# 36 products of a tile of ones on TensorE at the start of a two-layer gated attention kernel on one core

## Chip, core and metric

The kernel runs on one core of one Trainium2 chip. The metric is the device time in microseconds (us), median of three runs.

## The reference, cut to what matters

Eight sequences of 112 tokens (256 wide) go through two blocks; each block adds gated cross attention on a context of 375 rows and then a gated feed-forward part. All data are float32.

```python
x = x + tanh(g_xattn[0]) * L0_xattn(ctx, layernorm(x), ...)   # 8 heads of 64, rotary keys
x = x + tanh(g_ffn[0])   * L0_ffn(layernorm(x), ...)          # 8 experts, top 2, plus a shared one
x = x + tanh(g_xattn[1]) * L1_xattn(layernorm(x), ctx, ctx)   # 16 heads of 16
x = x + tanh(g_ffn[1])   * L1_ffn(layernorm(x), ...)          # gated q, k, v mix, causal attention
return x
# inside L0_xattn, for each sequence (xn: normed context, ln: normed latents)
q = (ln @ Wq) * scale
k, v = split(concat([xn, ln]) @ Wkv)
out = softmax(q @ rope(k).T) @ v @ Wo
```

The change touches only what runs before the first product of the first block. Nothing that it computes is part of the result.

## The kernel before

The program is written out by hand, one instruction stream for each engine, with counted semaphores between them. The first block's attention runs sequence by sequence (`n`, 0 to 7) and, within one, in four steps of two heads.

What happens before TensorE (PE) first works, for sequence 0:

- SyncE (SP) issues the loads: x of sequence 0, its context (`cx`, 375 KB), `ident`, `affine`, then `wkv`, `wq`, `cos_t`, `sin_t` and x of sequence 1.
- GpSimd (POOL) fills constants; `ones` (128x128) is the first (line 393), each with an increment of `s_fill`.
- VectorE (DVE) takes the statistics of the context (line 881), POOL turns them into scales (lines 416 to 419), ScalarE (ACT) normalises the context into `hat` (line 576, a tile of the `arena` buffer).
- PE waits for `ident` and `affine` (`s_const`), then for `hat` and the normed latents. It transposes them in two groups of four (`l0_t1`, recorded at line 1362, the helper `T`): three of the context and one of the latents each. ACT evicts each group with two instructions (lines 586 and 588) into `kvin`.
- PE then makes the first key product (line 1406, into bank 5 to 7 of `ps`), the query products (line 1396) and two value products (line 1409), with a second key product between these.
- ACT copies the first keys (line 603), SP swaps their halves by four small DMAs (line 297), DVE applies the rotation (lines 915, 917, 918), and PE makes the first two score products (line 1448).

A product of float32 operands stands in the trace as two records, a transpose as one. So the two instructions of a key product are four records, and the eight of a query product are sixteen.

The bank `ps[:, 4, :]` is used by the attention outputs (`l0_pv`, line 1468) for the first time in step 2 of sequence 0; its first product there has `start=True`. PE's beginning before the change:

```python
def T(dst, src, k):
    return pe.transpose(dst, src, ident[0:k, 0:k])

pe.wait_ge(s_const, 32)
```

Of the kernel before, what the change touches and what calls it, by code (L numbers as in the profile page):

```python
# [13 lines left out]
P = 128  # L14
# [34 lines left out]
def build(nc, a, out, xs, ys):  # L49
    ctx = ExitStack()  # L50
    with ctx:
        def sb(name, shape, dt=F32):
            return ctx.enter_context(nc.sbuf_tensor(name, shape, dt))

        def sem(name):
            return ctx.enter_context(nc.semaphore(name))

        ps = ctx.enter_context(nc.psum_tensor("ps", [P, 8, 512], F32))
# [8 lines left out]
        ones = sb("ones", [P, P])  # L67
# [139 lines left out]
        s_fill = sem("constants_made")  # L207
# [1152 lines left out]
        def _(pe):  # L1360
            def T(dst, src, k):
                return pe.transpose(dst, src, ident[0:k, 0:k])  # L1362

            pe.wait_ge(s_const, 32)

            def l0_t1(n, p):
# [521 lines left out]
                f_out(t)  # L1888


N_SMALL, N_FILL = 16, 8

L1_ROWS = ((), (), (0, 1), (), (2, 3), (4, 5), (6, 7), ())

# [101 lines left out]
```

## Time and profile before

| what | us |
|---|---|
| median of 3 runs | 807.23 |
| lowest and highest of them | 804.37, 810.54 |
| the profiled execution | 806.53 |
| its span | 804.7 |
| PE busy in it | 752.2 (93%) |

The profiled execution lies 0.70 us below the median. Its span leaves out 1.83 us around it. An interval of the trace is written start:end, in us from the span's start. Where the rows below give a granted clock, 1.00 stands for TensorE's full 2.4 GHz and 0.50 for 1.2 GHz.

### The profile page before, as it was taken

The numbers are of one execution on the slowest core, as the hardware profiler recorded it, in microseconds if no ns is written. First come the engines' busy times: TensorE is split into PE (matmuls) and PEld (weight loads), VectorE is DVE, ScalarE is ACT, GpSimd is POOL, SyncE is SP. The second block draws the span as 40 slices with busy tenths as digits, with TensorE's granted clock in tenths as the row PEclk, the third lists the DMA queues.
The fourth block names the chain that finished last, engine by engine and source line by source line (L and its number), as shares of the span: only waits on it lengthen the run. The fifth ranks groups of instructions, "written<-read, shape, count | busy, mean of one in ns | idle before, by whom it ended". The sixth has DMA issues, their size and how long they took to land.

```text
span 804.7 us, 14480 instructions
## 1 busy us (share of the span) xinstructions
PE 752.2 (93%) x5152; PEld 553.4 (69%) x5152; DVE 446.2 (55%) x1136; ACT 371.8 (46%) x991; POOL 182.4 (23%) x301
## 2 busy tenths in 40 slices
PE   3889999999999999999999999998999988999998
PEld 1355555555564666698889888666676767889976
DVE  1657758667666331122122221857788788698741
ACT  2456656556565621132332232467787878211210
POOL 2212112112100026000000001754446535411000
PEclk9999999999999999899999999999999999999999
DMA  4422224233121394155645542260000000000001
GB/s 137 113 56 60 73 78 149 68 113 83 36 55 38 94 353 179 61 173 212 228 163 175 187 139 84 73 220 2 2 2 2 2 2 2 1 1 1 0 12 35
DMA packets 43451, 69.74 MB, mean 87 GB/s; under 512 B 6531, under 2 KB 34956, under 8 KB 43124
## 3 DMA queue, kind: packets, MB, share of 16 engines
q1 hardware_dynamic: 41844, 65.14, 25.4%
q0 software_dynamic: 1536, 3.67, 1.5%
q8 instruction: 42, 0.69, 0.3%
q14 instruction: 29, 0.24, 0.1%
HBM read 52.56 MB, written 8.26 MB: 76 GB/s over the span
## 4 chain that ended last, share of the span: by engine, by line
PE 73%; DVE 9%; DMA 6%; ACT 5%; issue 4%; POOL 2%; SPq 1%; ACTq 0%; DVEq 0%
PE ps L1362 10%; PE ps L1595 7%; PE ps L1607 7%; PE ps L1813 7%; PE ps L1406 6%; PE ps L1409 6%; DMA OT<-slot_rows 4%; PE ps L1526 4%; PE ps L1850 3%; PE ps L1448 3%; PE ps L1695 3%; PE ps L1515 3%; PE ps L1468 3%; PE ps L1396 2%; PE ps L1419 2%
## 5 line engine op out<-in xcount | busy, mean ns | idle before, releaser
L1362 PE MATMUL ps<-ident,arena 112*122 112x112 f32 (+5 forms) x584 | 82.9, 276 | 21.2 <-ACT arena L576 13.7
L732 ACT ACTIVATE OT<-ps,bt 128x128 f32<-128x128 f32 x168 | 47.9, 368 | 114.2 <-PE ps L1595 113.3
L1362 PEld LDWEIGHTS ps<-ident,arena 112*122 112x122 f32 (+5 forms) x584 | 63.8, 155 | 46.1 <-issue 27.7
L1595 PE MATMUL ps<-OT,arena 128*128 128x128 f32 x672 | 80.5, 279 | 0.2 <-DVE OT L1076 0.2
L1595 PEld LDWEIGHTS ps<-OT,arena 128*128 128x128 f32 x672 | 78.7, 196 | 0.6 <-issue 0.6
L927 DVE TENSOR_REDUCE negmax<-ps 112x1 f32<-112x375 f32 x128 | 61.1, 539 | 30.4 <-PE ps L1695 30.3
L1813 PE MATMUL ps<-arena_r 128*112 128x384 f32 x384 | 75.9, 346 | 1.9 <-DVE acc L1164 1.0
L1607 PE MATMUL ps<-arena,OT 128*128 128x256 f32 x336 | 75.8, 379 | 0.0
L922 DVE TENSOR_REDUCE negmax<-ps 112x1 f32<-112x487 f32 x64 | 39.4, 657 | 56.8 <-PE ps L1448 56.6
L1090 DVE COPY yo<-ps 128x256 f32<-128x256 f32 x21 | 8.9, 424 | 108.3 <-PE ps L1607 108.3
L1607 PEld LDWEIGHTS ps<-arena,OT 128*128 128x128 f32 x336 | 62.3, 190 | 7.6
L1813 PEld LDWEIGHTS ps<-arena_r 128*112 128x112 f32 x384 | 63.8, 175 | 4.0 <-DVE arena L1304 1.2
L1406 PE MATMUL ps<-arena 128*128 128x487 f32 x128 | 61.3, 603 | 1.3 <-ACT arena L588 1.3
L1409 PE MATMUL ps<-arena 128*122 128x512 f32 x128 | 60.2, 592 | 0.0
L618 ACT ACTIVATE arena<-ps,negmax 112x487 f32<-112x487 f32 x64 | 42.6, 666 | 37.5 <-DVE negmax L922 37.5
L1304 DVE SCALAR_TENSOR_TENSOR arena<-ps,rw,arena 112x192 f32<-112x192 f32 x112 | 41.6, 412 | 11.5 <-PE ps L1813 9.7
L1409 PEld LDWEIGHTS ps<-arena 128*122 128x122 f32 x128 | 23.6, 185 | 29.5 <-issue 29.5
L774 ACT ACTIVATE arena<-ps,negmax 112x375 f32<-112x375 f32 x64 | 35.8, 572 | 11.5 <-DVE negmax L927 11.4
L1468 PEld LDWEIGHTS ps<-arena 122*64 122x64 f32 x512 | 24.7, 136 | 18.9 <-issue 18.5
L454 POOL COPY bt<-upb 128x8 f32 x21 | 3.9, 191 | 146.1 <-ACT OT L732 146.1
L1448 PE MATMUL ps<-arena 64*112 64x487 f32 x128 | 34.4, 614 | 2.5 <-DVE arena L918 2.5
L1406 PEld LDWEIGHTS ps<-arena 128*128 128x128 f32 x128 | 23.4, 199 | 18.3 <-issue 17.9
(269 smaller groups left out, 1373.6 us busy)
## 6 DMA issues: line engine op xcount, KB each, us to landing
arena<-in_up_w SPq DMA_DIRECT2D x21, 1024.0 KB, 5.1
arena<-in_down_w SPq DMA_DIRECT2D x8, 1024.0 KB, 11.9
arena<-arena SPq DMA_DIRECT2D x128, 60.9 KB, 2.0
arena<-in_wqkv SPq DMA_DIRECT2D x1, 3072.0 KB, 10.4
arena<-in_ctx SPq DMA_DIRECT2D x8, 375.0 KB
slot_rows<-acc SPq DMA_DIRECT2D x3, 896.0 KB, 5.0
OT<-slot_rows SPq DMA_DIRECT2D x21, 128.0 KB, 5.0
slot_out<-yo SPq DMA_DIRECT2D x21, 128.0 KB, 1.7
```

The source lines that it names most:

```text
L618: act.activation(probs[:, h % 4, 0:NK0], ps[0:TQ, h % 2, 0:NK0], ACT.Exp, bias=negmax[0:TQ, h % 2:h % 2 + 1], accum_out=rsum[0:TQ, h % 4:h ...
L732: act.activation(he[:, i % 2, m, :], ps[:, 2 * (i % 2) + m // 4, (m % 4) * SLOT:(m % 4 + 1) * SLOT], ACT.Gelu, bias=bt[:, i % 3, m:m + 1]) ...
L927: dve.tensor_reduce(negmax[0:TQ, h % 4:h % 4 + 1], ps[0:TQ, S_BANKS[h % 4], 0:TK], AX, ALU.max, negate=True)\
L1304: ins = dve.scalar_tensor_tensor(m, src, rwe(n, 2 * g + o), m, ALU.mult, ALU.add)
L1362: return pe.transpose(dst, src, ident[0:k, 0:k])
L1406: ins = pe.matmul(ps[:, bank, 0:NK0], wkv[:, c, j * P:(j + 1) * P], kvin[p][:, c, 0:NK0], start=(c == 0), stop=(c == KC - 1))
L1409: ins = pe.matmul(ps[0:KP0, bank, :], kvin[p][:, c, j * KP0:(j + 1) * KP0], wkv[:, c, 512:1024], start=(c == 0), stop=(c == KC - 1))
L1448: pe.matmul(ps[0:TQ, r, 0:NK0], qh[p][rows, u, :], kr[rows, u, 0:NK0], start=True, stop=True, tile_position=(64 * r, 0)).then_inc(L0["s"], 1)
L1468: ins = pe.matmul(ps[64 * k:64 * k + 64, 4, (h // 2) * TQ:(h // 2 + 1) * TQ], v0[p][:, j, (h + k) * DH0:(h + k + 1) * DH0], pT[:, (g + k) ...
L1595: ins = pe.matmul(ps[:, 2 * (i % 2) + m // 4, (m % 4) * SLOT:(m % 4 + 1) * SLOT], wu[i % 3][:, c, m * P:(m + 1) * P], xgT[:, i % 2, c, :], ...
L1607: ins = pe.matmul(ps[:, 4 + i % 2, 0:D], he[:, i % 2, m, :], wdc[i % 2][:, m, :], start=(m == 0), stop=(m == FM - 1))
L1813: ins = pe.matmul(ps[0:TQ, g % 4, 0:384], xv[p][:, c, :], wv[:, c, 2 * g:2 * g + 2, :].rearrange("p e n -> p (e n)"), start=(c == 0 and k ...
```

## The change

PE waits until the tile `ones` is filled, and then multiplies it by itself 36 times into the first 128 columns of bank 4, each product with `start=True` and `stop=True`; nothing reads the result. Only then does it wait for `ident` and `affine` as before. Every other engine's program is unchanged.

```diff
@@ -1361,6 +1361,9 @@
             def T(dst, src, k):
                 return pe.transpose(dst, src, ident[0:k, 0:k])
 
+            pe.wait_ge(s_fill, 1)
+            for i in range(N_WARM):
+                pe.matmul(ps[:, 4, 0:P], ones[:, :], ones[:, :], start=True, stop=True)
             pe.wait_ge(s_const, 32)
 
             def l0_t1(n, p):
@@ -1888,7 +1891,7 @@
-N_SMALL, N_FILL = 16, 8
+N_SMALL, N_FILL, N_WARM = 16, 8, 36
```

On PE, the program's first rows before the change, with the semaphores that each waits for (`consts_loaded` is `s_const`, `ctx_normed` is `s_hat`, `l0_t1e` counts ACT's evictions into `kvin`, `w_l0_loaded` is the load of `wkv`):

```order
L1359 UNCONDITIONAL_BRANCH [waits barrier_Pool_Activation_PE_DVE_SP_release]
L1362 MATMUL ps<-ident,arena 128x125 [waits latents_normed,ctx_normed,consts_loaded]
L1362 MATMUL ps<-ident,arena 128x125 x2
L1362 MATMUL ps<-ident,xn 128x112
L1362 MATMUL ps<-ident,arena 128x125 x3
L1362 MATMUL ps<-ident,xn 128x112
L1406 MATMUL ps<-arena 128x487 [waits l0_t1e,w_l0_loaded]
```

The same place in the changed kernel, where `constants_made` is `s_fill` and later lines are numbered three higher:

```order
L1359 UNCONDITIONAL_BRANCH [waits barrier_Pool_Activation_PE_DVE_SP_release]
L1366 MATMUL ps<-ones 128x128 [waits constants_made]
L1366 MATMUL ps<-ones 128x128 x35
L1362 MATMUL ps<-ident,arena 128x125 [waits latents_normed,ctx_normed,consts_loaded]
L1362 MATMUL ps<-ident,arena 128x125 x2
L1362 MATMUL ps<-ident,xn 128x112
L1362 MATMUL ps<-ident,arena 128x125 x3
L1362 MATMUL ps<-ident,xn 128x112
L1409 MATMUL ps<-arena 128x487 [waits l0_t1e,w_l0_loaded]
```

The 36 products stand ahead of the first transpose; between the transposes and the key product (line 1406, now 1409) nothing is added, and the rest of PE's order is unchanged.

## Rows read from the trace of the kernel before

**Rows 1.** The page: span, granted clock in 40 slices, the chain by engine.
```profile
span 804.7 us, 14480 instructions
...
PEclk9999999999999999899999999999999999999999
...
PE 73%; DVE 9%; DMA 6%; ACT 5%; issue 4%; POOL 2%; SPq 1%; ACTq 0%; DVEq 0%
```

**Rows 2.** Chain that ended last, from the start: start us, us, what.
```profile
1.20 6.12 DMA arena<-in_ctx
...
10.95 1.59 ACT arena L576 x3
...
12.63 1.06 PE ps L1362 x4
...
13.78 0.66 ACT arena L586
...
15.33 0.34 ACT arena L588
...
15.81 3.58 PE ps L1406 x4
19.39 2.00 PE ps L1396 x16
```

**Rows 3.** Timeline: start us, us, engine, line, operation, out<-in, count, idle before and releaser.
```profile
0.74 0.20 POOL L393 MEMSET ones<- 128x128 f32 x1 [0.29 <-POOLq L1987]
...
19.43 0.58 ACT L603 ACTIVATE arena<-ps 128x487 f32<-128x487 f32 x1 [3.77 <-PE ps L1406]
...
24.03 0.67 DVE L917 TENSOR_TENSOR arena<-arena,sin_t 128x487 f32<-128x487 f32 x1 [3.25 <-DMA arena<-arena]
...
24.73 0.67 DVE L918 TENSOR_TENSOR arena<-arena 128x487 f32<-128x487 f32 x1
```

**Rows 4.** Timeline of PE alone, 19 to 27 us.
```profile
19.19 2.21 PE L1396 MATMUL ps<-arena 128*128 128x112 f32 x16
21.23 1.89 PE L1409 MATMUL ps<-arena 128*122 128x512 f32 x4
22.96 1.80 PE L1406 MATMUL ps<-arena 128*128 128x487 f32 x4
24.59 1.88 PE L1409 MATMUL ps<-arena 128*122 128x512 f32 x4
26.41 1.07 PE L1448 MATMUL ps<-arena 64*112 64x487 f32 x4
```

**Rows 5.** Stretches: start:end, length, PE busy (records), granted clock, DMA share, GB/s.
```profile
15.80:19.40 3.60, 3.59 (x6) 1.00 0.00 0
...
48.00:49.00 1.00, 1.00 (x4) 0.50 0.00 0
...
340.00:341.00 1.00, 1.00 (x8) 0.69 0.00 0
```

**Rows 6.** The chain that ended last, at three later places.
```profile
48.28 2.80 PE ps L1406 x4
...
75.73 2.04 PE ps L1396 x16
77.77 1.65 PE ps L1406 x4
...
336.58 5.73 PE ps L1595 x32
...
349.78 3.57 PE ps L1595 x32
```

**Rows 7.** Timeline of PE alone, 40 to 49 us.
```profile
40.65 0.54 PE L1362 MATMUL ps<-ident,arena 125*128 125x125 f32 x3 [1.10 <-ACT arena L576]
41.03 0.26 PE L1362 MATMUL ps<-ident,xn 112*128 112x112 f32 x1
...
45.72 2.56 PE L1396 MATMUL ps<-arena 128*128 128x112 f32 x16 [2.17 <-ACT arena L588]
```

## The prediction

> **What bounds the kernel now.** I read the page first. PE holds 73% of the chain that ended last, so work taken off PE, or PE work done faster on that chain, comes off the time almost in full [rows 1]. I then followed the chain from the start. It doesn't touch PE for 12.6 us: the context's load takes 6.12 us, statistics and normalising end at 12.54 (10.95 + 1.59), and only at 12.63 does PE begin its transposes. They hold the chain for 1.06 us, ACT's four evictions for 1.89 us (13.78 to 15.67, which is 15.33 + 0.34), then the key and query products for 5.58 us [rows 2]. So PE stands idle ahead of 12.63, nothing that depends on PE can be early there, and work put into that hole is free if it ends by 12.63.
>
> The second thing to see is how long those first products take. The first key product is four records of 128x487. From its start to the start of the query product it takes 3.38 us (15.81 to 19.19) [rows 2, 4]; the next one, of the same form, takes 1.63 us (22.96 to 24.59) [rows 4]. That is a ratio of 2.07, that of the two levels 2.4 and 1.2 GHz. The granted clock in that stretch reads 1.00 [rows 5], so here the durations must be believed and not the column: a later pair agrees, since the same product takes 2.80 us where the column says 0.50 (at 48 us) and 1.65 us elsewhere [rows 5, 6]. The query product behind it takes 2.04 us from start to start (19.19 to 21.23) [rows 4]. At full clock, the same group takes 2.04 us including the tail of its last record [rows 6]; that tail is about 0.16 us, since the next records start at such a distance ahead of the end elsewhere (0.20 at 19.19 against 19.39) [rows 2, 4]. So about two of its sixteen records were still slow, and the clock rose near 19.5. PE had then transposed for 1.5 us, idled 1.3 us and multiplied for 3.7 us.
>
> **The change part by part.** It removes nothing. It adds one wait and 72 records (36 float32 products of two records each) of 128x128. `ones` is filled at 0.94 [rows 3], so PE starts near 1.0.
>
> Their cost at full clock is taken from the up product, also 128x128: 3.57 / 32 = 0.112 us each [rows 6]. Below full clock I take the first such group, which is 5.73 us with the clock low until about 340.6 (a granted 0.69 over one us is 0.62 us at one half and the rest at full) [rows 5, 6]: 4.0 us low; the other 1.7 us hold 15 records; so 17 records in 4.0 us, 0.24 us each with the first one's start. Twice 0.112 would be 0.22. I take 0.23.
>
> When does the clock rise? The trace gives two bounds: 3.7 us after the first product (15.81 to 19.5) and 6.9 us after the first transpose (12.63 to 19.5). With 3.7: 16 records to 4.7 us, the other 56 take 6.3, end at 11.0. With 6.9: 30 records to 7.9 us, the other 42 take 4.7, end at 12.6. Both end at or before 12.63, so the 36 products lie in the hole. They write bank 4, which no other engine reads before PE's own attention products reset it, so nothing waits for them but PE.
>
> The gain, if the clock stays up until PE has real work again, is three terms. First, the transposes: the same group of four at full clock takes 0.64 us (40.65 to 41.29, which is 41.03 + 0.26) [rows 7] against 1.06 [rows 2], so 0.42 less. The second group's saving is hidden, since ACT is the one waited for there: 1.89 us of evictions stand ahead of 15.81 in either kernel. Second, the key product: 3.38 − 1.63 = 1.75 us. Third, the query product: 2.04 − 1.88 = 0.16 us. Sum: 2.33 us.
>
> Is it kept? The next join is the first score product at 26.41, which waits for the rotated keys. Those end at 25.40 (24.73 + 0.67), 5.39 us after ACT's copy of the key product (19.43 + 0.58 = 20.01) [rows 3]. The copy moves by 0.42 + 1.75 = 2.17, so the keys are ready at 23.23, and PE arrives at 26.41 − 2.33 = 24.08 [rows 4]. PE is still last, with 0.85 us to spare. The swap DMAs and the later loads on SP are queued behind that same copy and move with it. From there on the whole program slides.
>
> So the span becomes 802.4 and the time, with the 1.83 us around it, 804.2. The profiled execution lies 0.70 below the median, which puts the same gain at 804.9 there. I take 804.5.
>
> A rule of the Trainium skill speaks against keeping the clock up. On PE between 11.0 or 12.6 and 15.4 there are only eight transposes (1.0 us at full clock) and idle time. What the trace shows is mixed. After 1.10 us idle, PE transposes at 40.65 at full speed; but after 2.17 us idle, at 45.72, the query product takes 2.56 us and the key product behind it 2.80 [rows 6, 7], with the column at 0.50 [rows 5]. So the clock does fall here, after a hole shorter than the one that remains behind the 36 products. (The skill's "TensorE: Matmul & The Clock Gate", Part 4, says that transposes don't count as activity of PE, and its table under "Why this matters for your kernels" that a long enough gap between bursts of products brings the low clock back. By these the hole would be one piece from the end of the 36 products to 15.4, the first key product would run at 1.2 GHz again, and the time would be 806.1 in place of 804.2. The fall at 47 us agrees with the second rule; no row tells the two kinds of instruction apart.)
>
> **The rivals.**
>
> *A, forecast (0.57).* Clock up from the transposes to the query product: 804.2 to 804.9.
>
> *B, the clock falls again before or in the first key product (0.30).* For it speaks the fall near 47 us; against it, that PE had idled in several places in the 10 us ahead of that fall, and had not just been busy for ten. Price: the transposes' 0.42 us may stay, the other 1.91 us go, so 806.1; if the transposes are slow too, 806.5, and if the fall comes so early that the clock is back within the key product, some 805.3.
>
> *C, the products of ones don't raise the clock, or it rises late (0.07).* This ends on the other side. All 72 records at 0.23 us take 16.6 us, to 17.6, and the first transpose starts 5.0 us late: 806.5 + 5.0 = 811.5, or 809.2 if the clock then is up. It decides when the clock rises later than t, with t + (72 − (t − 1)/0.23) × 0.112 = 12.63 + 2.33 = 14.96; that is t = 12.6 us (with rise at t, the delay eats the gain). The trace's later bound, 7.9, is far from this, hence the small chance. A clock fully up changes little: at 0.112 they would end at 9.1.
>
> *D, the later dips move (0.06 alone, and as spread around A to C).* The dip near 47 costs 0.52 (2.56 against 2.04) + 1.15 (2.80 against 1.65) = 1.67 us; the one near 336 costs 5.73 − 3.57 = 2.16 us [rows 6, 7]. A start 2.3 us earlier puts different work under the moments at which the clock changes. With A and both gone: 800.4; with A and one more of 1.7: 805.9, with B and one more: 807.8.
>
> **How the numbers follow.** The forecast is A at 804.5. Its own range is 802.5 to 806.5 (one dip more or less). To leave out no more than 2 in 10, the range takes in B with a dip more (807.8) and A with both dips gone (800.4, cut to 801): 801.0 to 808.0. C lies outside it. One per cent, about what a measurement of this kernel can tell from no change (its three runs span 6.2 us), is 8.1 us: faster means under 799.2, slower over 815.3. Even A with both dips gone reaches only 800.4, and C's worst 811.5. Only the spread of the runs on top of them gets past the bounds: 0.04 faster, 0.02 slower, 0.94 the same.
>
> **What would show it.** In the profile after: 72 records of the line with `ones` on PE from about 1.0, ending between 11 and 12.7 (C: beyond 13); first transpose still at 12.6; ACT's first eviction at 13.3 to 13.4; key product starting near 15.4 and lasting 1.6 to 1.8 us (B: 3.4 and, if the column then reads right, 0.50); first value product at 18.9 in place of 21.23; first score product near 24.1 in place of 26.41. If the key product is fast and the score product is not earlier by over 2 us, the step on the rotated keys is wrong. If that is earlier and the end isn't, the gain was given back further on: the granted clock near 47 and 336 tells whether by D.

## The result

| | kernel before | changed kernel |
|---|---|---|
| median of 22 runs | 806.02 us | 803.56 us |
| lowest to highest | 801.58 to 813.36 | 800.95 to 805.71 |
| profiled execution, span | 804.7 us | 800.4 us |
| ratio, with 95% interval | | 0.9965 (0.9949 to 0.9981) |

The change makes the kernel 0.35% faster, that is 2.8 us (1.5 to 4.1), and the medians differ by 2.5 us. The prediction was 804.5 us in a range of 801.0 to 808.0, with "the same within 1%" as the likeliest case. The ratios leave out executions that took over 1.5% more than the fastest of their kernel; of the changed kernels that is a single one, of 1497.77 us, among the nine of the second series of this kernel (below), of which there is no trace and whose cause is open.

The page of the changed kernel, span and granted clock in 40 slices, to be read beside [rows 1]:

```profile
span 800.4 us, 14624 instructions
...
PEclk9999999999999999899999999999999999999999
```

TensorE's timeline of the changed kernel (start us, us, engine, line, operation, out<-in, count, idle before and its releaser), the counterpart of [rows 4] and [rows 7]. Lines from 1366 on stand three higher than before:

```profile
1.00 10.53 PE L1366 MATMUL ps<-ones 128*128 128x128 f32 x72 [1.00 <-POOL mhalf L394]
12.56 0.51 PE L1362 MATMUL ps<-ident,arena 125*128 125x125 f32 x3 [1.03 <-ACT arena L576]
...
15.29 1.87 PE L1409 MATMUL ps<-arena 128*128 128x487 f32 x4 [1.71 <-ACT arena L588]
17.00 1.93 PE L1399 MATMUL ps<-arena 128*128 128x112 f32 x16
18.77 1.89 PE L1412 MATMUL ps<-arena 128*122 128x512 f32 x4
...
23.94 1.07 PE L1451 MATMUL ps<-arena 64*112 64x487 f32 x4
...
43.26 3.65 PE L1399 MATMUL ps<-arena 128*128 128x112 f32 x16 [2.17 <-ACT arena L588]
...
48.39 1.88 PE L1412 MATMUL ps<-arena 128*122 128x512 f32 x4
```

The products of ones end at 11.53, 1.0 us ahead of the first transpose. The first key product takes 1.87 us in place of 3.58, and the first score product starts at 23.94 in place of 26.41. In this execution the whole hole before 12.6 came 0.08 us earlier for another reason (the context's load), so the change moved the score product by 2.39 us.

The chain that ended last, from the start (counterpart of [rows 2]):

```profile
12.56 0.62 PE ps L1362 x4
...
13.26 0.66 ACT arena L586
...
15.29 1.87 PE ps L1409 x4
17.17 1.77 PE ps L1399 x16
```

Stretches of the changed kernel (start:end, length, PE busy with its records, granted clock, DMA share, GB/s), counterpart of [rows 5]:

```profile
1.00:5.70 4.70, 4.70 (x22) 1.00 0.52 145
5.70:11.50 5.80, 5.80 (x52) 1.00 0.97 337
...
43.00:46.00 3.00, 2.75 (x13) 0.54 0.08 26
...
330.00:336.00 6.00, 4.49 (x20) 0.50 0.01 3
```

PE runs 22 records in 4.7 us and then 52 in 5.8: 0.214 us each and then 0.112. The granted clock reads 1.00 in both, since the column shows nothing lower until the clock has changed once. So the clock rose at 5.7 us. Both later dips are still there, at 43 and 330 us. They begin 3.8 us earlier than before, while the work around them has moved by 2.5 and 4.0 us, and they hit the same products: from the query product to the value product behind the first dip it is 5.13 us (43.26 to 48.39), against 5.20 before (45.72 to 50.92).

The spans of the two profiled executions differ by 4.3 us, more than the change gives. Aligned record by record, PE's stream is 2.5 us earlier at 50 us, 3.2 us at 137 us (the start of a query product) and 4.0 us at 199 us (again one), and 4.3 at the end. At 137 us, the chain before goes through VectorE's statistics of a context (line 881), which stand ahead of the maximum that ACT waits for; after the change they are earlier. But the same two steps, 0.6 us at 137 and 0.8 us at 199, stand between the trace of before and every other trace of this document, also the one with 54 products, whose stream is only 0.1 us earlier than before's at 130 us, and the one with products over 9 rows, whose stream is 2.8 us later there. So the earlier start doesn't make them; what does stays open. The whole 1.9 us is within what single executions of one kernel differ by (5 us above), and the timed runs don't show it.

### The profile page after: what moved, and what is told of

Same layout as the page of the kernel before. It is cut to its first block, busy times and chain, and to the rows that moved or that the text cites. A ratio compares the mean times of both kernels' runs of the same rounds, so it can differ in the third digit from the quotient of the medians.

```text
span 800.4 us, 14624 instructions
## 1 busy us (share of the span) xinstructions
PE 760.2 (95%) x5224; PEld 562.9 (70%) x5224; DVE 446.2 (56%) x1136; ACT 371.7 (46%) x991; POOL 181.6 (23%) x301
## 4 chain that ended last, share of the span: by engine, by line
PE 74%; DVE 8%; DMA 5%; ACT 5%; issue 4%; POOL 2%; SPq 1%; ACTq 0%; DVEq 0%
PE ps L1362 10%; PE ps L1598 7%; PE ps L1816 7%; PE ps L1610 6%; PE ps L1412 6%; PE ps L1409 6%; DMA OT<-slot_rows 4%; PE ps L1451 4%; PE ps L1529 4%; PE ps L1853 3%; PE ps L1698 3%; PE ps L1518 3%; PE ps L1471 3%; PE ps L1399 2%; PE ps L1422 2%
## 5 line engine op out<-in xcount | busy, mean ns | idle before, releaser
L1409 PE MATMUL ps<-arena 128*128 128x487 f32 x128 | 58.4, 579 | 1.7 <-ACT arena L588 1.7
L1304 DVE SCALAR_TENSOR_TENSOR arena<-ps,rw,arena 112x192 f32<-112x192 f32 x112 | 41.6, 412 | 11.5 <-PE ps L1816 9.7
L774 ACT ACTIVATE arena<-ps,negmax 112x375 f32<-112x375 f32 x64 | 35.8, 572 | 11.5 <-DVE negmax L927 11.4
L626 ACT ACTIVATE arena<-ps 122x448 f32<-122x448 f32 x64 | 34.0, 549 | 2.3 <-PE ps L1362 2.3
```

Source lines behind the costliest of these rows:

```text
L1304: ins = dve.scalar_tensor_tensor(m, src, rwe(n, 2 * g + o), m, ALU.mult, ALU.add)
L1409: ins = pe.matmul(ps[:, bank, 0:NK0], wkv[:, c, j * P:(j + 1) * P], kvin[p][:, c, 0:NK0], start=(c == 0), stop=(c == KC - 1))
```

## The experiments

All of them are edits of the changed kernel; ratios are to the kernel before, on the same chip. Chips differ by more than the change (medians of the kernel before from 806.0 to 811.2 us), so only ratios and traces are compared. The kernels with 36 transposes, with 18 late products, with products over 9 rows, with the wide bias rows alone and with six more products (first of two series) ran once each: their traces count, their times tell nothing. Lines of `kernel.py` stand a few higher or lower from one kernel to the next.

### Fewer products: does the clock stay up over a longer hole?

```diff
-N_SMALL, N_FILL, N_WARM = 16, 8, 36
+N_SMALL, N_FILL, N_WARM = 16, 8, 18
```

> The changed kernel with 18 products of ones in place of 36, all else the same. They are 36 records: with the clock rising near 5 us they end near 7.3 us, and PE then idles for over 5 us ahead of its first transpose at 12.6. Theory 1 (what matters is whether the clock is still up when real work begins, and a long idle hole brings it down): transposes and first key product at 1.2 GHz again, the key product about 3.4 us, the first score product at 26.2 to 26.4, the time as before the change (ratio 1.000). Theory 2 (once the clock has risen it stays up over this hole): the key product takes 1.87 us, the score product stands at 24.0, ratio 0.997 as with 36, and half of the products do nothing.

TensorE's timeline of the kernel with 18 products:

```profile
1.00 6.21 PE L1366 MATMUL ps<-ones 128*128 128x128 f32 x36 [1.00 <-POOL mhalf L394]
12.62 0.86 PE L1362 MATMUL ps<-ident,arena 125*128 125x125 f32 x3 [5.41 <-ACT arena L576]
...
15.80 3.32 PE L1409 MATMUL ps<-arena 128*128 128x487 f32 x4 [1.32 <-ACT arena L588]
...
25.89 1.07 PE L1451 MATMUL ps<-arena 64*112 64x487 f32 x4
```

A stretch of it (columns as above):

```profile
11.90:18.70 6.80, 4.76 (x12) 0.50 0.02 7
```

Theory 1 holds in the trace. After 5.4 us idle, the clock was back at 1.2 GHz, here shown by the column too. The transposes are as slow as without any product of ones, and the key product nearly so (3.32 us against 3.58). The score product starts at 25.89, 0.5 us earlier than before and 0.3 us earlier than I had expected, since the clock came back sooner, at 18.7 us, just ahead of the query product. The ratio, 0.9978 (0.9945 to 1.0012), fits 1.000 and can't rule out 0.997. The mean granted clock of the timed executions speaks for theory 1: 0.984 over these twelve, 0.990 over the fifteen of the kernel before on the same chip; the fall of 6.8 us alone makes 0.004 of that.

### More products: what an overrun costs

```diff
-N_SMALL, N_FILL, N_WARM = 16, 8, 36
+N_SMALL, N_FILL, N_WARM = 16, 8, 54
```

> The changed kernel with 54 products of ones in place of 36. The products lie in a hole that ends at 12.56; 36 of them end at 11.5. 36 more records of 0.112 us end at 15.5, so the first transpose starts 3.0 us later than with 36, and everything behind it too: first score product at 26.9, time 3.0 us over the kernel with 36, which is +0.5 us against the kernel before, ratio 1.000 to 1.001. The rival, that the delay is hidden by some slack further on, gives 0.997.

TensorE's timeline of the kernel with 54 products:

```profile
1.00 14.17 PE L1366 MATMUL ps<-ones 128*128 128x128 f32 x108 [1.00 <-POOL mhalf L394]
15.01 0.48 PE L1362 MATMUL ps<-ident,arena 125*128 125x125 f32 x3
...
26.37 1.07 PE L1451 MATMUL ps<-arena 64*112 64x487 f32 x4
```

The first transpose starts at 15.01, behind the products, 2.45 us later than with 36, and the score product 2.43 us later. So nothing hides an overrun, and the score product stands where it was before the change (26.41): the whole gain is spent. It stays so further on: at 130 us PE's stream is 0.1 us earlier than before, against 2.5 us with 36 products. I had written 3.0 us, because I had let the products end at 15.5; the clock rose 0.7 us earlier in this execution. The timing doesn't decide: the interval of the ratio, 0.9975 (0.9949 to 1.0002), holds the rival's 0.997 and only just 1.000.

### Transposes in place of products

```diff
-                pe.matmul(ps[:, 4, 0:P], ones[:, :], ones[:, :], start=True, stop=True)
+                pe.transpose(ps[:, 4, 0:P], ones[:, :], ident2[:, :])
```

with `ident2`, a second copy of the identity tile, loaded from ACT's queue at the program's start, and PE waiting for it.

> The changed kernel with 36 transposes of the tile of ones (one record each) in place of 36 products; so that they can start early, a second copy of the identity tile is loaded from ACT's queue, and they start when it lands, near 4 us. Theory T (transposes don't count as activity for TensorE's clock, as the Trainium skill says in its page TensorE: Matmul & The Clock Gate, Part 4): all 36 take 0.21 us each to the end, near 11.7 us, and the key product takes 3.4 us. Rival (any busy PE counts): the transposes change from 0.21 to 0.11 us each within 7 us, and the key product takes 1.9 us.

Its partner keeps that load and that wait, and makes 18 products.

> The partner of the run with 36 transposes: the same second load of the identity tile and the same start near 4 us, but 18 products of ones (36 records as well). The clock rises within the stretch (records change from 0.23 to 0.112 us each), they end near 10 us, and the key product takes 1.9 us, whatever holds for transposes. If the key product is slow here too, the pair tells nothing of transposes, but that the hole of 2.5 us behind the products is too long.

TensorE's timeline with 36 transposes:

```profile
3.14 6.61 PE L1370 MATMUL ps<-ident,ones 128*128 128x128 f32 x36 [3.14 <-DMA ident<-in_ident]
...
15.23 3.48 PE L1413 MATMUL ps<-arena 128*128 128x487 f32 x4 [1.71 <-ACT arena L591]
```

Its stretches:

```profile
3.00:8.00 5.00, 4.86 (x23) 1.00 0.80 242
8.00:10.00 2.00, 1.75 (x15) 1.00 1.02 394
10.00:15.00 5.00, 1.03 (x8) 1.00 0.34 120
15.00:18.50 3.50, 3.27 (x4) 0.51 0.00 0
```

TensorE's timeline with 18 products from 3.28 us on:

```profile
3.28 6.98 PE L1370 MATMUL ps<-ones 128*128 128x128 f32 x36 [3.28 <-DMA ident<-in_ident]
12.79 0.86 PE L1365 MATMUL ps<-ident,arena 125*128 125x125 f32 x3 [2.52 <-ACT arena L579]
...
15.96 3.48 PE L1413 MATMUL ps<-arena 128*128 128x487 f32 x4 [1.32 <-ACT arena L591]
```

One stretch of it:

```profile
12.00:13.00 1.00, 0.21 (x1) 0.69 0.17 61
```

The transposes raised the clock: 23 of them in 4.9 us, then 15 records in 1.75. That speaks against theory T: in this kernel transposes over all 128 rows do count. The Trainium skill says ("TensorE: Matmul & The Clock Gate", Part 4: PE-mode transpose) that transposes don't count as busy in the same way; the measurement decides. I had expected the late products to hold the clock up over their 2.5 us of idle time, and they didn't. It fell near 12.4, the transposes ran slowly, and the key product took 3.48 us. After the 36 transposes (2.7 us idle) it stayed up for the real transposes and fell at about 15.1, ahead of the key product. So the length of the first idle time alone doesn't decide when the clock falls: it was down by the end of 2.5 us in one of the two executions and not after 2.7 us in the other. In both, an end at about 10 us was too early for the key product; one at 11.5 to 11.7 was enough twice and once not (below).

### Products over 9 rows

```diff
-                pe.matmul(ps[:, 4, 0:P], ones[:, :], ones[:, :], start=True, stop=True)
+                pe.matmul(ps[:, 4, 0:P], ones[0:9, :], ones[0:9, :], start=True, stop=True)
```

> The changed kernel with the 36 products of ones over 9 rows of the tile in place of 128 (operands 9x128), so that PE is as busy by the profile with a small part of its array. The question is raised by the dip near 330 us, which comes right behind products over 9 rows while PE reads as fully busy. Theory R (few rows count little): the 72 records stay at 0.21 to 0.23 us each, end near 17 us, the first transpose is 4.6 us late, and the key product takes 3.4 us at 1.2 GHz. Rival (only the time that PE is busy counts): 0.11 us each from 5 to 8 us on, end near 11.5, key product 1.9 us.

TensorE's timeline of the kernel with products over 9 rows:

```profile
1.00 15.72 PE L1366 MATMUL ps<-ones 9*128 9x128 f32 x72 [1.00 <-POOL mhalf L394]
16.65 0.89 PE L1362 MATMUL ps<-ident,arena 125*128 125x125 f32 x3
...
19.86 3.58 PE L1409 MATMUL ps<-arena 128*128 128x487 f32 x4 [1.32 <-ACT arena L588]
...
30.90 1.07 PE L1451 MATMUL ps<-arena 64*112 64x487 f32 x4
```

Theory R holds: PE reads as busy for 15.7 us on end, the records stay at 0.22 us, and the key product behind them still takes 3.58 us. This is also what rival C would have looked like: first transpose 4.0 us late (4.6 expected), first score product at 30.90 (4.5 us late). The time of this one execution, 808.5 us, lies within the kernel before's on that chip (806.8 to 820.3) and tells nothing.

### The changed kernel once more

> The changed kernel as it is, once more on this chip, as the yardstick of the runs beside it and a second profile of it: ratio to the kernel before 0.997 (the shift of 2.4 us counted at the first score product), key product at full clock again if 36 products are enough whatever the moment at which the chip looks; 3.4 us if that depends on it.

No edit. Ratio 0.9950 (0.9925 to 0.9975), from eight of nine executions, in agreement with 0.9965. In its profile, the products end at 11.74, and the clock was up over the second hole here too:

```profile
15.26 1.87 PE L1409 MATMUL ps<-arena 128*128 128x487 f32 x4 [1.71 <-ACT arena L588]
```

The score product starts at 23.91.

### The bias products over 128 rows

```diff
-        wT = sb("wT", [E0 + 1, TOK])
+        wT = sb("wT", [P, TOK])
...
-        dnb = sb("dnb", [E0 + 1, D])
+        dnb = sb("dnb", [P, D])
...
+            pool.memset(wT[:, :], 1.0).then_inc(s_pad, 1)
+            pool.memset(dnb[:, :], 0.0).then_inc(s_pad, 1)
```

The two fills follow POOL's `latents_rstd(0, 1)`. The loads into `dnb` and ACT's copies into rows 0 to 8 of `wT` wait for them.

> The changed kernel with the product that adds the down biases (line 1530 in the kernel before, operands of 9 rows) widened to 128 rows: the other 119 rows hold ones on one side and zeros on the other and add nothing; two fills on POOL near 12 us are added. Records and columns are the same in number. If the clock fell at 333.8 and 330.0 us because products over 9 rows count little (as the run with 9 rows at the start suggests), the dip of 6.8 us there is gone and the first up product of the experts (32 records) takes 3.6 us in place of 5.7. The rival, that the hole of 1.6 us behind these products brings the clock down, keeps the dip.

TensorE's timeline of the changed kernel near its second dip:

```profile
325.38 0.68 PE L1533 MATMUL ps<-dnb,wT 9*112 9x256 f32 x2
325.99 0.69 PE L1529 MATMUL ps<-wbuf,OT 128*112 128x256 f32 x2
...
331.32 1.09 PE L1362 MATMUL ps<-ident,OT 128*128 128x128 f32 x4 [1.58 <-DVE acc L1069]
332.59 5.81 PE L1598 MATMUL ps<-OT,arena 128*128 128x128 f32 x32 [0.18 <-DVE OT L1076]
```

The same place in the kernel with wide bias rows, whose lines are numbered five higher:

```profile
325.29 0.59 PE L1534 MATMUL ps<-wbuf,OT 128*112 128x256 f32 x2
325.72 0.59 PE L1538 MATMUL ps<-dnb,wT 128*112 128x256 f32 x2
...
329.62 0.63 PE L1367 MATMUL ps<-ident,OT 128*128 128x128 f32 x4 [1.58 <-DVE acc L1074]
330.64 3.81 PE L1603 MATMUL ps<-OT,arena 128*128 128x128 f32 x32 [0.39 <-DVE OT L1081]
```

The first key product of the same execution:

```profile
15.83 3.20 PE L1414 MATMUL ps<-arena 128*128 128x487 f32 x4 [1.72 <-ACT arena L592]
```

And a stretch of it:

```profile
16.30:19.60 3.30, 3.30 (x8) 0.50 0.00 0
```

The dip is gone, though the idle time ahead of the experts' first transposes is still 1.58 us: up product 3.81 us in place of 5.81. So the few rows brought it about; the hole alone doesn't. All eleven profiled executions without the wide rows, the kernel before's among them, have the dip there, and none of the three with them has it. I had not expected the second gain: a pair of bias and down products took 1.23 us (0.61 each from start to start) and takes 0.86 with 128 rows. There are two stretches of such pairs: the one from 297 to 302 us is 1.35 us shorter with the wide rows, and this one 1.27 us.

The same execution shows rival B: with 36 products that ended at 11.7 us, the clock fell at about 16.2, within the key product, which took 3.20 us. The real transposes came 0.5 us later here (13.08) than in the kernel without the fills. The next fall came at 40.1 us, ahead of the second query product's hole.

### The holes filled

```diff
             l0_t1(0, 0)
+            for i in range(6):
+                pe.matmul(ps[:, 4, 0:P], ones[:, :], ones[:, :], start=True, stop=True)
             pe.wait_ge(s_w0, 16)
```

> The changed kernel with 6 more products of ones (12 records) between the transposes and the first key product, in the idle 1.7 us there. In the profile after the change the key product already runs at full clock, so the theory that the 36 products alone hold the clock over this hole expects no change: 1.3 us of products that end by 15.1, key product at 15.29 for 1.87 us. The rival, that the hole makes the clock fall in some executions, would show only over many, so a single look can show just that the filling costs nothing.

> The changed kernel with 6 products of ones between the transposes and the first key product, timed. With 36 products alone, two profiles kept the clock up over this hole and a third, whose transposes came 0.5 us later, lost it at 16.2 us, within the key product, at a cost of 1.9 us. If the clock falls there in a third of the executions, filling the hole gains 0.6 us on average, which is below what the timing can tell: ratio 0.995 to 0.997, as with 36 products alone on other chips. If it falls in most of them, 0.993.

Both expectations are for this one edit. In the first execution the six products end at 14.6 and the key product starts at 14.96 for 1.87 us: they cost nothing. (It starts 0.3 us earlier than with 36 alone because the transposes do, at 12.22.) In the profile of the second series it takes 1.87 us too. Timed over seven executions, the ratio is 0.9909 (0.9875 to 0.9944), below the 0.995 to 0.997 that I held likelier; only the other case, that the clock falls there in most executions (0.993), lies within the interval. Against that case stand two profiles of three with 36 products alone, in which the clock stayed up. The interval also meets that of the changed kernel on another chip (0.9925 to 0.9975). The mean granted clock of the timed executions speaks against it too: it is 0.9916 with the filling and 0.9911 (22 executions) and 0.9908 (8) without, where a fall of 3.4 us in every execution would lower it by 0.0021. What the filling is worth on average stays open.

Both holes, that is the above and:

```diff
+                        if n == 0:
+                            for i in range(9):
+                                pe.matmul(ps[:, 4, 448:512], ones[:, :], ones[:, 0:64], start=True, stop=True)
                         l0_q(n + 1, q)
```

> The changed kernel with 6 more products of ones between the transposes and the first key product, and 9 products of 64 columns (18 records, some 2 us) in the idle 2.17 us ahead of the second query product (near 41 us), into columns that nothing reads. If the dip of the clock there (3.4 us at 1.2 GHz, which costs 1.7 us) comes from that hole, it is gone: query product 2.0 us in place of 3.65, and the time 1.7 us under the kernel with 36 products, ratio to the kernel before near 0.995. If it isn't the hole, the dip stays and the time is that of the kernel with 36, 0.997.

TensorE's timeline of the kernel with both holes filled:

```profile
40.64 2.13 PE L1497 MATMUL ps<-ones 128*128 128x64 f32 x18
42.99 2.04 PE L1399 MATMUL ps<-arena 128*128 128x112 f32 x16 [0.21 <-ACT arena L588]
```

A later stretch of it:

```profile
300.00:303.00 3.00, 3.00 (x5) 0.52 0.62 242
```

The query product takes 2.04 us in place of 3.65, so with the hole filled the first dip is gone; the two kernels below that fill it have none near 45 us either. In nine of the other profiled executions the clock fell at the end of that hole or up to 1.4 us behind it. In two it fell earlier, at 45.2 (products over 9 rows at the start, whose stream runs late) and at 40.1 us (wide bias rows), each time at an idle time of 1.1 us ahead of the transposes. So this hole brings the clock down where it is still up, but the clock can also fall ahead of it. From the query product's start to the value product's it is 3.52 us (42.99 to 46.51), against 5.13 with 36 products alone: 1.6 us. Part of it can be given back: in this execution the clock fell at 300 us instead, behind the first stretch of products over 9 rows, and PE's stream, 5.9 us earlier than before at 290 us, is only 4.2 us earlier at 320. Ratio 0.9919 (0.9885 to 0.9953): it holds the 0.995 that I expected and not 0.997, but it isn't below the 0.9909 with only the first hole filled, so the timing doesn't show the second filling's 1.6 us.

### Both holes and the wide rows

> The kernel that fills both idle holes (6 products ahead of the first key product, 9 ahead of the second query product) and has the bias products over 128 rows. Expected: no stretch at 1.2 GHz near 45 us nor near 330 us; 1.7 us and 2.5 us less than the kernel with 36 products alone, ratio to the kernel before 0.992. If the widening does nothing: 0.995.

> As the kernel that fills both holes and has the bias products over 128 rows, but its two fills on POOL wait until the first query product is done (near 19 us), where POOL and VectorE are idle. In the run before, the fills stood at 12 us and the first transposes came 0.7 us late, behind VectorE's normalising of the latents, which took longer beside them. Expected: transposes back at 12.3 to 12.6 us, first score product 0.7 us earlier, no stretch at 1.2 GHz near 45 or 330 us, ratio to the kernel before 0.988. If the fills weren't the reason, the transposes stay near 13.2 and the ratio at 0.989.

The edits are those above; in the second of the two, the fills on POOL stand behind `pool.wait_ge(L0["q"], 1)`. POOL's timeline with the early fills:

```profile
11.87 0.84 POOL L426 MEMSET wT<- 128x896 f32 x1
```

VectorE's timeline of the same kernel:

```profile
11.96 1.15 DVE L903 TENSOR_SCALAR xn<-xn,mv,rstd 112x256 f32<-112x256 f32 x1 [2.00 <-POOL rstd L414]
```

VectorE's timeline with the late fills:

```profile
11.50 0.41 DVE L904 TENSOR_SCALAR xn<-xn,mv,rstd 112x256 f32<-112x256 f32 x1 [1.99 <-POOL rstd L414]
```

Two stretches of the kernel with the late fills:

```profile
50.00:650.00 600.00, 576.96 (x4092) 1.00 0.33 105
650.00:690.00 40.00, 34.63 (x340) 0.96 0.01 2
```

On the clock and on the fills both expectations hold, and the ratios meet theirs within the intervals, the first at its very edge. Neither execution has a stretch at 1.2 GHz from 8 to 650 us. The mean granted clock of the timed executions agrees: 0.9973 and 0.9968 over six each, against 0.9908 and 0.9916 for the kernels on the same chips that have both dips. But both profiled executions have a dip of 3.4 us near 672 us, as the kernel with the wide rows alone has and the kernel before and the first profile of the changed one have not (of the others, two have one at 681 us and one at 658), and PE's stream loses 1.5 us there. Beside POOL's fill, VectorE's normalising takes 1.15 us in place of 0.41, and moved away the fill costs nothing: the transposes start at 12.29 in place of 13.26. The ratios are 0.9892 (0.9864 to 0.9920) and 0.9849 (0.9804 to 0.9895). So the best version measured is 1.5% (1.1 to 2.0) faster than the kernel before, where the change alone gives 0.35% (0.50% on another chip). On their own chips, the two kernels are each 0.6% below the one with the 36 products alone (0.9950) and the one with the first hole filled (0.9909). What the traces show for it adds up to about 9 us: 2.4 from the change, 1.6 from the second query product, 2.0 from the first up product, 2.6 from the two stretches of bias and down products, and 0.3 from the transposes ahead of the up product (1.27 to 1.02 from start to start). That is 1.1%, at the edge of the interval, and 0.9% if the dip near 672 us, with its 1.5 us, comes with the edits; so not all of the 1.5% is accounted for.

## Why the prediction was right

**What bounds the start.** Right. PE depends on nothing but its own order ahead of 12.6, and products in the hole cost nothing as long as they end in it. The run with 54 products gives the price beyond: all that overruns is paid.

**The cost of the 72 records.** I bounded the rise between 4.7 and 7.9 us and the end between 11.0 and 12.6. In ten profiles of kernels that start with products of ones over 128 rows near 1.0 us, it rose at 5.0 to 7.1 us; with 36 of them they end at 11.4 to 12.2. The fast record is 0.112 us, as taken; the slow one is 0.213, where I had taken 0.23 from a group that also held a start-up.

**The gain.** Three terms, 0.42 + 1.75 + 0.16 = 2.33. Measured on the chain: transposes 1.06 to 0.62 (0.44); key product from start to start 3.38 to 1.71 (1.67); query product 2.04 to 1.77 (0.27). Sum 2.38, and 2.39 at the score product. So the key product gave slightly less than I took and the query product slightly more: I had allowed a full-clock query product 1.88 us, and this one takes 1.77. The forecast of 804.5 lies 0.9 us above the measured 803.56, mostly because it was reckoned from three executions of the kernel before, with a median of 807.23; from the 806.02 of 22 executions the same 2.33 us give 803.7.

**Is it kept?** Right. The rotated keys are ready at 23.18 (22.51 + 0.67), and the score product starts at 23.94, so PE stays last with 0.76 us to spare, against 0.85 worked out. VectorE's last step in the changed kernel:

```profile
22.51 0.67 DVE L918 TENSOR_TENSOR arena<-arena 128x487 f32<-128x487 f32 x1
```

**Rival B** was a real risk, and the forecast owes something to where the products end. With an end at 7.2 (18 products), 9.8 (36 transposes) or 10.3 us (18 late ones), the clock was down before the key product; with 11.5 to 11.7 it stayed up twice and fell once. My chance of 0.30 fits that, on three executions, and that the profiled one was among the two is in part luck. The trace of before had the reason in it: the fall near 47 us behind a 2.2 us hole. The three profiles with that hole filled, which have no dip there, show what the hole does.

**Rival C** needed products that don't count. Products of ones over all rows do; products over 9 rows don't. I had priced it at 5.0 us, and that run shows 4.0 to 4.5. (The moment at which a late rise eats the gain works out at 12.5 us from the terms given, not 12.6; nothing hangs on it.)

**Rival D** didn't occur as such: both dips stayed with their work in the changed kernel, and cost about what they cost before. What I had wrong is the cause of the second. I treated the dips as a matter of moments; the one near 330 us sits behind products over 9 rows, whether the kernel starts earlier or not. The one execution with both holes filled and a dip at 300 us shows that a rival of this kind exists.

## What to carry to other kernels

An idle stretch before the first real work can raise TensorE's clock for nothing, but what counts is that the filling ends shortly before that work and that the holes behind it are short or filled too. Here 18 products did next to nothing, 36 gave 2.4 us where the clock stayed up (two profiles of three), and with 54 the overrun was paid in full. When the granted clock dips in the middle of a kernel, look at what PE did just before: an idle hole (fill it) or products over a few rows (widen them with padding), even where PE reads as busy. And don't trust a granted clock of 1.00 before the first change on record: compare the duration of one form early and late.

## What the runs showed of the hardware that I had not expected

- Transposes over 128 rows raise the clock like products: 0.213 us each from 3.14 us on, 0.11 from 8.2 us on.
- Products over 9 rows don't raise it in 15.7 us without a gap. Alternating with products over 128 rows in the middle of the kernel, they are what brings it down there.
- Products over 9 rows that alternate with ones over 128 rows cost 0.61 us a step where the same steps over 128 rows cost 0.43, at full clock in both. The cause stays open.
- A fill of 0.84 us on POOL that began 0.1 us ahead of a VectorE operation stretched it from 0.41 to 1.15 us, in both profiles that have them side by side. In the profile shown the operation ended 0.40 us behind the fill (13.11 against 12.71), about the time that it takes alone.
